# Down product of an expert layer: the 64-row half in three products of 128 rows, two of them stacked

## The reference

```python
gu = jnp.einsum('ech,eoh->eco', xb, gate_up_proj)     # 48 experts, 192 slots of 512
g, u = jnp.split(gu, 2, axis=-1)                      # 192 and 192
h = jax.nn.silu(g) * u
out = jnp.einsum('eci,ehi->ech', h, down_proj)        # 192 slots x 512
...
final = jnp.zeros_like(x).at[tok].add(y * w[:, None])
```

## Time and profile before

| what | value |
|---|---|
| runs | 1069.98, 1064.69, 1068.07 us; median 1068.07 |
| the profiled execution | 1064.81 us, of which the span from first to last instruction is 1063.1 |
| busy over the span | PE 96%, DVE 79%, ACT 59%, POOL 53% |
| mean granted TensorE clock | 0.986 of full speed |
| down products L1426, high x low, 128-row left side | 391 ns each |

### The profile page before, as it was taken

How to read it: one execution, slowest core, us unless ns; L and a number is a source line. 1 busy time by engine, 2 the same in 40 slices (tenths; PEclk the granted TensorE clock), 3 DMA queues, 4 the chain that set the end, 5 groups by cost and what they waited for, 6 DMA issues and landing times.

```text
span 1063.1 us, 24370 instructions
## 1 busy us (share of the span) xinstructions
PE 1016.1 (96%) x6564; PEld 835.6 (79%) x6564; DVE 835.3 (79%) x2255; ACT 624.7 (59%) x1751; POOL 560.9 (53%) x565
## 2 busy tenths in 40 slices
PE   5999799999999999999999997899999999999994
PEld 4787687887887887887877875688888888888883
DVE  5777587887887887888888876378888888888883
ACT  4555455555545545545555553177777777777772
POOL 3225466566567666666666666623443434434334
PEclk9999899999999999999999999799999999999998
DMA  7999584453331221211311514168999999999995
GB/s 274 376 306 254 209 292 183 145 213 138 101 116 50 77 72 50 87 61 50 98 50 50 210 40 159 41 207 236 255 261 248 263 251 256 262 241 263 252 224 69
DMA packets 90644, 185.75 MB, mean 175 GB/s; under 512 B 23943, under 2 KB 24071, under 8 KB 89712
## 3 DMA queue, kind: packets, MB, share of 16 engines
q1 hardware_dynamic: 59232, 145.13, 42.6%
q0 software_dynamic: 31376, 40.20, 16.8%
HBM read 116.04 MB, written 122.00 MB: 224 GB/s over the span
## 4 chain that ended last, share of the span: by engine, by line
PE 54%; issue 13%; POOL 13%; DMA 9%; DVE 8%; ACT 1%; SPq 1%; DVEq 1%; POOLq 0%; ACTq 0%
PE ps L1236 15%; PE ps L1392 14%; PE ps L1426 9%; POOL slot_records L594 7%; PE ps L1221 5%; DMA arena<-in_x 4%; PE ps L1408 3%; PE ps L1226 3%; POOL rstd L605 2%; DVE qk_both L1058 2%; DMA arena<-slot_records 2%; DMA layer_out<-qk_both,slot_table 2%; POOL arena L650 1%; PE ps L1334 1%; PE ps L1263 1%
## 5 line engine op out<-in xcount | busy, mean ns | idle before, releaser
L594 POOL DMA_INDIRECT slot_records<-row,slot_idx x240 | 243.3, 1014 | 80.2 <-issue 50.8
L679 POOL DMA_INDIRECT layer_out<-qk_both,slot_table x96 | 145.1, 1511 | 218.2 <-DMA layer_out<-qk_both,slot_table 190.7
L605 POOL TENSOR_TENSOR rstd<-mv,neg_half 128x1 f32<-128x1 f32 x96 | 67.8, 706 | 125.5 <-DVE mv L976 78.6
L1236 PE MATMUL ps<-w_high,xn_high 128*128 128x512 f32 x384 | 114.1, 419 | 0.7 <-ACT xn_high L700 0.7
L735 ACT ACTIVATE arena<-ps,neg_max 128x128 f32<-128x128 f32 x256 | 89.9, 377 | 31.9 <-DVE neg_max L968 31.9
L1236 PE MATMUL ps<-w_high,xn_low 128*128 128x512 f32 x384 | 107.3, 401 | 0.0
L1236 PE MATMUL ps<-w_low,xn_high 128*128 128x512 f32 x384 | 107.2, 401 | 0.0
L700 ACT ACTIVATE xn_t<-ps 128x512 f32<-128x512 f32 x64 | 38.3, 599 | 100.8 <-PE ps L1221 100.7
L1392 PE MATMUL ps<-w_high,w_low 128*128 128x192 f32 x576 | 87.8, 274 | 0.0
L1392 PE MATMUL ps<-w_low,w_high 128*128 128x192 f32 x576 | 87.7, 274 | 0.0
L1392 PE MATMUL ps<-w_high 128*128 128x192 f32 x576 | 86.8, 272 | 0.4 <-DVE w_low L1143 0.4
(11 more groups left out here) (164 smaller groups left out, 2468.5 us busy)
## 6 DMA issues: line engine op xcount, KB each, us to landing
gu_sb<-in_gate_up SPq DMA_DIRECT2D x48, 768.0 KB, 5.4
slot_records<-arena SPq DMA_DIRECT2D x6, 3366.0 KB, 25.1
arena<-slot_records SPq DMA_DIRECT2D x48, 280.5 KB, 4.8
dn_sb<-in_down_proj SPq DMA_DIRECT2D x48, 256.0 KB, 5.4
arena<-in_x SPq DMA_DIRECT2D x32, 256.0 KB, 2.7
x_res<-in_x SPq DMA_DIRECT2D x32, 256.0 KB, 3.0
ctx_t_sb<-in_ctx_t SPq DMA_DIRECT2D x32, 256.0 KB, 3.5
ctx_sb<-in_ctx_rows SPq DMA_DIRECT2D x32, 256.0 KB, 4.0
```

The lines of the kernel that those rows point to most:

```text
L594: pool.indirect_dma_start(out=records, out_offset=bass.IndirectOffsetOnAxis(ap=slot_idx_of(s)[:, k:k + 1], axis=0), in_=row_of(s), in_offs ...
L605: pool.tensor_tensor(rstd[:, :], mv[:, 1:2], neg_half[:, 0:1], ALU.pow).then_inc(steps.sem, 1)
L679: pool.indirect_dma_start(out=out, out_offset=bass.IndirectOffsetOnAxis(ap=slot_table[0:PART[h], 2 * d.index + h:2 * d.index + h + 1], axi ...
L1236: last = pe.matmul(dst, left[:, c, :], right[:, m, c, :], start=(n == 0 and c == 0), stop=(n == 2 and c == KC - 1))
```

## The change

Three things change, all in the expert stage.

- **Products.** The second half of the down product takes three products instead of five. `h1_low` and a second copy of the last 64 columns of `h1_high` lie side by side, as do the high and low parts of `h2`, and 128 columns that reach across the seam (`MIXED`) are the left side. So the product with `dn_high` gives low x high in the rows 0 to 63 of bank 5 and high x high in the rows 64 to 127. The two halves of that bank must be added. ScalarE scales the rows 64 to 127 into a spare part of `y` (`y1_rest`), and VectorE scales the rows 0 to 63 and adds them (`scalar_tensor_tensor`).
- **Copies.** ScalarE writes the 64 columns of `h1_high` a second time (`high1_again`), VectorE subtracts the low part of `h2` in two pieces, and copies the 64 slot weights to the rows 64 to 127.
- **Order.** The split of the 64-row down weights (ScalarE's `dn2_high`, VectorE's `dn2_low`) moves from the end of the turn in which the expert is `u` to the turn in which it is `d`, between the first and the second silu.

```diff
@@ -243,16 +243,20 @@
+                                  (P, 2, 1, 2 * CAP + P)):
+        gu_high, rows_high, dn_high, dn2_both, h1_parts = split_buffers(w_high)
+        gu_low, rows_low, dn_low, _, h2_parts = split_buffers(w_low)
+        LEFT = (slice(2 * CAP - P, 2 * CAP), slice(CAP, 2 * CAP - P))
+        MIXED = slice(P, 2 * CAP - P)
         HALVES = (slice(0, INTER - P), slice(INTER - P, P))
+        h1_low, h1_high_again = h1_parts[:, :, :, 0:CAP], h1_parts[:, :, :, CAP:2 * P]
+        h1_high = h1_parts[:, :, :, 2 * P:2 * P + CAP]
+        h2_high, h2_again = h2_parts[HALVES[0], :, :, 0:CAP], h2_parts[HALVES[1], :, :, 0:CAP]
@@ -809,6 +813,13 @@
                     if u.back(1).exists():
                         act.wait_ge(gup_v.sem, gup_v.after(u.back(1), "h2"))
                     act.activation(silu1[:, :], ps[:, 2, 0:CAP], ACT.Silu).then_inc(gup_a.sem, 1)
+                if d.exists():
+                    if d.first():
+                        act.wait_ge(d_dn2, 16 * 3)
+                    if d.back(2).exists():
+                        act.wait_ge(dwn_t.sem, dwn_t.after(d.back(2), "y1"))
+                    copy(dn2_high(d), dn2_raw(d), wdn_a)
+                if u.exists():
                     act.wait_ge(gup_t.sem, gup_t.after(u, "second"))
                     act.activation(silu2[:, :], ps[0:INTER - P, 3, 0:CAP], ACT.Silu).then_inc(gup_a.sem, 1)
                 if t.exists():
@@ -824,6 +835,8 @@
                     for h, dst, name in ((h1, h1_high, "h1"), (h2, h2_high, "h2")):
                         act.wait_ge(gup_v.sem, gup_v.after(u, name))
                         copy(dst[:, u.parity, 0, :], h[:, :], gup_a)
+                        if name == "h1":
+                            copy(h1_high_again[:, u.parity, 0, :], h1[:, P:CAP], gup_a)
                     copy(h2_again[:, u.parity, 0, :], h2[:, :], gup_a)
                 if d.exists():
                     act.wait_ge(dwn_t.sem, dwn_t.after(d, "y0"))
@@ -831,16 +844,16 @@
                     if d.back(2).exists():
                         act.wait_ge(d_add[d.back(2).parity], moved(d.back(2), 2))
                     copy(y[:, d.parity, 0, :], ps[:, 4, :], dwn_a, scale=weight_of[d.parity][:, 0:1])
+                    act.wait_ge(dwn_t.sem, dwn_t.after(d, "y1"))
+                    copy(y[PART[1]:P, d.parity, 1, :], ps[PART[1]:P, 5, :], dwn_a,
+                         scale=weight_of[d.parity][PART[1]:P, 1:2])
                 if n.exists():
                     split_gate_up(n)
                 if u.exists():
                     act.wait_ge(d_dn[u.parity], moved(u, 1))
-                    if u.first():
-                        act.wait_ge(d_dn2, 16 * 3)
                     if u.back(2).exists():
                         act.wait_ge(dwn_t.sem, dwn_t.after(u.back(2), "y1"))
                     copy(dn_high[:, u.parity, 0, :], dn_sb[:, u.parity, :], wdn_a)
-                    copy(dn2_high(u), dn2_raw(u), wdn_a)
             expert_turns(act, expert_turn)
 
         @block.vector
@@ -1151,6 +1164,10 @@
                         dve.wait_ge(gup_v.sem, gup_v.after(u.back(1), "low2"))
                         dve.wait_ge(gup_a.sem, gup_a.after(u.back(1), "again"))
                     dve.tensor_tensor(h1[:, :], silu1[:, :], ps[:, 2, CAP:2 * CAP], ALU.mult).then_inc(gup_v.sem, 1)
+                if d.exists():
+                    dve.wait_ge(wdn_a.sem, wdn_a.after(d, "high2"))
+                    left_by(dn2_low(d), dn2_raw(d), dn2_high(d)).then_inc(wdn_v.sem, 1)
+                if u.exists():
                     dve.wait_ge(gup_a.sem, gup_a.after(u, "silu2"))
                     dve.tensor_tensor(h2[:, :], silu2[:, :], ps[INTER - P:P, 3, 0:CAP], ALU.mult)\
                         .then_inc(gup_v.sem, 1)
@@ -1170,20 +1187,24 @@
                     dve.wait_ge(gup_a.sem, gup_a.after(u, "high2"))
                     if u.first():
                         for parity in range(2):
-                            dve.memset(h2_rest[HALVES[1 - parity], parity, 0, :].bitcast(FP32), 0.0)
-                    left_by(h2_low(u), h2[:, :], h2_high[:, u.parity, 0, :]).then_inc(gup_v.sem, 1)
-                if d.exists():
-                    dve.wait_ge(dwn_t.sem, dwn_t.after(d, "y1"))
-                    dve.wait_ge(ffn_w.sem, ffn_w.after(d, "weight"))
-                    if d.back(2).exists():
-                        dve.wait_ge(d_add[d.back(2).parity], moved(d.back(2), 2))
-                    dve.tensor_scalar(y[0:PART[1], d.parity, 1, :], ps[0:PART[1], 5, :],
-                                      weight_of[d.parity][0:PART[1], 1:2], None, ALU.mult).then_inc(dwn_v.sem, 1)
+                            dve.memset(h2_parts[HALVES[1 - parity], parity, 0, CAP:2 * CAP].bitcast(FP32), 0.0)
+                    for h in range(2):
+                        left_by(h2_low(u, h), h2[:, part(h)], h2_high[:, u.parity, 0, part(h)]).then_inc(gup_v.sem, 1)
                 if t.exists():
                     dve.wait_ge(d_rows[t.parity], moved(t, 2))
                     dve.tensor_copy(slot_table[:, bass.ds(2 * t.index, 2)],
                                     rows[:, t.parity, :, TOKEN:ROW].bitcast(I32).rearrange("p h o -> p (h o)"))\
                         .then_inc(ffn_w.sem, 1)
+                if d.exists():
+                    dve.wait_ge(dwn_a.sem, dwn_a.after(d, "y1_rest"))
+                    dve.wait_ge(dwn_t.sem, dwn_t.after(d, "y1"))
+                    dve.wait_ge(ffn_w.sem, ffn_w.after(d, "weight"))
+                    if d.back(2).exists():
+                        dve.wait_ge(d_add[d.back(2).parity], moved(d.back(2), 2))
+                    dve.scalar_tensor_tensor(y[0:PART[1], d.parity, 1, :], ps[0:PART[1], 5, :],
+                                             weight_of[d.parity][0:PART[1], 1:2], y[PART[1]:P, d.parity, 1, :],
+                                             ALU.mult, ALU.add).then_inc(dwn_v.sem, 1)
+                if t.exists():
                     if t.back(2).exists():
                         dve.wait_ge(dwn_a.sem, dwn_a.after(t.back(2), "y0"))
                         dve.wait_ge(dwn_v.sem, dwn_v.after(t.back(2), "y1"))
@@ -1191,6 +1212,9 @@
                     dve.tensor_copy(weight_of[t.parity][:, :],
                                     rows[:, t.parity, :, bass.ds(t.index + DM, 1)]
                                     .rearrange("p h o -> p (h o)")).then_inc(ffn_w.sem, 1)
+                    dve.wait_ge(ffn_w.sem, ffn_w.after(t, "weight0"))
+                    dve.tensor_copy(weight_of[t.parity][PART[1]:P, 1:2],
+                                    weight_of[t.parity][0:PART[1], 1:2]).then_inc(ffn_w.sem, 1)
                 if n.exists():
                     dve.wait_ge(wgu_a.sem, wgu_a.after(n, "high"))
                     if n.back(2).exists():
@@ -1201,8 +1225,6 @@
                     dve.wait_ge(wdn_a.sem, wdn_a.after(u, "high"))
                     left_by(dn_low[:, u.parity, 0, :], dn_sb[:, u.parity, :], dn_high[:, u.parity, 0, :])\
                         .then_inc(wdn_v.sem, 1)
-                    dve.wait_ge(wdn_a.sem, wdn_a.after(u, "high2"))
-                    left_by(dn2_low(u), dn2_raw(u), dn2_high(u)).then_inc(wdn_v.sem, 1)
             expert_turns(dve, expert_turn)
 
         @block.tensor
@@ -1419,12 +1441,18 @@
                         else:
                             if d.back(1).exists():
                                 pe.wait_ge(dwn_v.sem, dwn_v.after(d.back(1), "y1"))
-                        dst = ps[0:PART[h], 4 + h, :]
-                        pairs = [(h1_high, dn_high, P), (h1_high, dn_low, P), (h1_low, dn_high, P),
-                                 (h2_twice, dn2_both, P), (h2_rest, dn2_both, P)]
-                        for i, (left, right, n) in enumerate(pairs):
-                            last = pe.matmul(dst, left[0:n, d.parity, 0, part(h)], right[0:n, d.parity, 0, :],
-                                             start=(i == 0), stop=(i == len(pairs) - 1))
+                        e = d.parity
+                        if h == 0:
+                            steps = [(P, h1_high[:, e, 0, 0:P], dn_high), (P, h1_high[:, e, 0, 0:P], dn_low),
+                                     (P, h1_low[:, e, 0, 0:P], dn_high), (P, h2_parts[:, e, 0, 0:P], dn2_both),
+                                     (P, h2_parts[:, e, 0, LEFT[0]], dn2_both)]
+                        else:
+                            steps = [(P, h1_parts[:, e, 0, MIXED], dn_high),
+                                     (PART[1], h1_high[:, e, 0, P:CAP], dn_low),
+                                     (P, h2_parts[:, e, 0, MIXED], dn2_both)]
+                        for i, (n, left, right) in enumerate(steps):
+                            last = pe.matmul(ps[0:n, 4 + h, :], left, right[:, e, 0, :],
+                                             start=(i == 0), stop=(i == len(steps) - 1))
                         last.then_inc(dwn_t.sem, 1)
             expert_turns(pe, expert_turn)
 
```

16 lines of the change are left out of this document (6 added, 10 removed).

## The result

The changed kernel takes 1115.74 us (median of six runs, 1111.82 to 1117.23); the kernel before takes 1067.12 beside it (six runs, 1063.59 to 1069.98). The ratio is 1.045, with a 95% interval from 1.042 to 1.048: slower, as forecast, but by 48.6 us and not by 11. The time lies outside the predicted range.

The account below looks back on a forecast made before the run. A loop through D, down products, y1_rest and VectorE's subtractions, at 7.67 us, overtakes TensorE's pace: 45 x (7.67 - 7.353) = +14.3, + 0.4 - 3.5 = +11.2 us, giving 1079 us, 1.0% slower; range 1071 to 1097.

Parts of the forecast that it names:

- D: The moment VectorE ends the low part of the 64-row down weights; the prediction counts a turn's times from it.
- The first rival: Expert stage: TensorE's pace holds, the turn falls to 6.87 us and the time to 1046 us, faster; chance 8%.
- Two products fewer: TensorE's down products: two fewer at 0.23 us each save 0.46 us a turn; wider products cost nothing more.
- The release times: Waits between engines: the first down product starts 0.05 us after D, VectorE's gate-up subtraction 0.03 after ScalarE's split.
- the choice of the route: Ahead of VectorE's gate-up subtraction: ScalarE's split allows its start at 4.30 us, VectorE's own way at 4.22; ScalarE's taken.
- The spare of 0.31: Kernel before: the loop through D needs about 7.0 us against TensorE's 7.33, leaving about 0.31 us spare a turn.
- `y1_rest` from 2.20 to 2.89: ScalarE's added scaling takes 0.69 us, the next instruction starting after 0.59, so the gate-up split starts at 2.79.
- the predicted 7.67: Expert stage: the length in us of one turn of the loop after the change, against 7.353 before.
- The moved split: VectorE's turn end: gate-up subtraction 1.68 us, down subtraction 0.61, silu product 0.39 now in the loop, D's instruction 0.69.
- The end: Last additions into the output: POOL works off its lag in slower turns, 20.4 us instead of 24.0, a gain of 3.5.
- the loop is longer: Third rival, expert stage: short waiting VectorE instructions or TensorE's clock at 1.2 GHz make turns 8.2 us, 1103 us; chance 6%.

Follow-up runs that it names:

- e3: The changed kernel without ScalarE's y1_rest and the wait for it, rows 64 to 127 of bank 5 left out of the result: 1068.01 us, ratio 1.003.
- e10: The changed kernel with turns 24 to 47 of the expert stage written out with constants, turns 6 to 23 left in the hardware loop: 1097.97 us, ratio 1.028.
- e4: The changed kernel with only the order of waits changed ahead of the down products, y0 and y1, the last-released wait checked last: 1090.08 us, ratio 1.023.
- e2: The kernel before, its products kept, with only the split of the 64-row down weights moved between the silus: 1072.48 us, ratio 1.007.
- the last kernel: The changed kernel with down-weight split at turn's end, gate-up work ahead of y1, late waits last, all but two turns written out: 1077.18 us, ratio 1.009.

## Why the prediction was wrong in its size

*The bound and the direction: right.* TensorE's two products fewer gave nothing, and the loop through D, `y1_rest` and VectorE's subtractions became the bound. The first rival (1046) did not come. The rule that stood beside it, in the Trainium skill's "Perfetto Trace Analysis", section "Identifying the Most-Contended Engine", would have had the relief of the busiest engine pay; it did not pay here: the engine at 99.79% was relieved by 0.46 us a turn and the turn grew by 1.1. That is no test of the rule, since no run relieves TensorE without lengthening the loop; even without `y1_rest` (`e3`) the moved split and the copies are left, and the turn is 7.47.

*Two products fewer: right.* Behind the first step they stand 0.23 apart, 1.72 us from the first to the eighth (802.72, 804.44), and the wider ones are no slower.

*The release times: the step that failed.* "On release it starts 0.05 after D" was taken from the earlier trace rows, and the 0.03 between ScalarE's split and VectorE's subtraction from the earlier trace rows. Both are rows of written-out turns. In the hardware loop the same releases take 0.34 (TensorE) and 0.22 (VectorE's `y1`). `e10` shows both values in one trace, `e4` that the order of the waits alone changes them. What follows is that the gate-up subtraction starts at D + 4.94 and not at D + 4.30. With it the choice of the route failed: "ScalarE's is later and I take it" holds in the written-out turn, but in the loop each wait on VectorE adds to VectorE's own way (0.22 ahead of `y1`, 0.24 ahead of the weight copies), and that way, put at 4.22, ends at D + 4.91 while the split ends at D + 4.87. ScalarE adds its part, too: `y0` starts 1.62 behind the first product in the loop and 1.46 in the written-out turn. The spare of 0.31 was a misreading of the same kind: the product at 1036.79 in the earlier trace rows, of expert 45, is the first one behind the loop, where the release is short and the 0.36 is mostly spare. In the turns of the loop the step has nearly the same length (801.75 - 801.40 = 0.35), but there the release takes 0.34 of it. `e2` puts the true spare at 0.06.

*`y1_rest` from 2.20 to 2.89, with the next start after 0.59: too short.* It takes 0.69 as estimated, and in the written-out turn it ends at 948.95, D + 2.91. But the split starts 0.02 behind that end, at D + 2.93, and not 0.10 ahead of it at 2.79: the 0.59 of the earlier trace rows was taken from two instructions that both start in row 0, while `y1_rest` works on the rows 64 to 127 between two that start in row 0. The kernel before already shows the difference, in two of its turns (L700 on `arena` works on the rows 0 to 63 for an even expert and on the rows 64 to 127 for an odd one):

```profile
805.44 0.62 ACT L700 ACTIVATE w_high<-dn_sb 128x512 fp32r<-128x512 f32 x1
805.96 0.62 ACT L700 ACTIVATE w_high<-arena 64x512 fp32r x1
...
1032.97 0.62 ACT L700 ACTIVATE w_high<-dn_sb 128x512 fp32r<-128x512 f32 x1
1033.62 0.63 ACT L700 ACTIVATE w_high<-arena 64x512 fp32r x1
```

With the same start row the second starts 0.10 before the end of the first (805.96 against 806.06), with another start row 0.03 behind it (1033.62 against 1033.59). This is most of the 7.80 of `e10` beside the predicted 7.67. The prediction weighed the change of start rows for VectorE and not for ScalarE.

*The moved split: right.* From the gate-up subtraction on, 1.68, 0.60, 0.38 and 0.69 were measured for 1.68, 0.61, 0.39 and 0.69. The rule of the Trainium skill's "VectorE: DVE Perf Modes", section "Two Vector instructions with no wait between them", by which an instruction that starts in another group of 32 rows is held until those before it have finished, agrees: with the same start rows the silu product starts 809.60 - 809.00 = 0.60 after a subtraction of 0.69, with other ones D's subtraction starts 0.38 after a silu product of 0.34.

*The end: wrong.* The gain of 3.5 us did not come. POOL still waits for its own additions (206.7 us in 40 waits), the additions behind expert 45 are issued 1089.60 - 1085.84 = 3.76 after the end of `y0`, and from there to the end it is 1110.0 - 1085.84 = 24.16 us against 24.0 before. In the kernel before expert 45's were issued 1042.83 - 1039.12 = 3.71 after its `y0`, so the slower turns let POOL work nothing off: its additions became slower with the turn. Why was not tried.

*The rivals.* The third one, "the loop is longer", is the nearest to what came, but only in part by its mechanisms. The falls of the clock it names gave 5 us. Of the short VectorE instructions that wait for the one before, the wait of 0.24 ahead of the weight copies is in the loop, 0.11 more than in the written-out turn. The slow releases on TensorE, ScalarE and VectorE, the largest part, it does not name. It had 6% and 8.2 us a turn; the loop alone takes 8.36.

The sum, against the profiled execution (1111.82 against the predicted 1076.0, 35.8 more): the loop's releases 45 x (8.36 - 7.80) = 25.2, the overlap on ScalarE that isn't there, 45 x (7.80 - 7.67) = 5.9 (what the written-out turn already has), the falls 5.0, the end 3.7, less 3.1 for a first `y0` that ends at 704.87 + 0.69 = 705.56, that much earlier than forecast: 36.7. The 0.9 too much fits the first and last turns, which are written out and mostly shorter than 8.36. The 3.1 says nothing of the change: in the traces here the first down product starts anywhere between 702.8 and 708.3.

What stays open: which part of the release is the checking of the waits and which is work on registers, since `e4` changed the order and `e10` both the waits' form and the registers; why the clock fell in these four turns and not in others with the same waits; and what binds the last kernel.

## What to carry to other kernels

Take the time from a release to the start of an instruction from the turns that repeat, never from the written-out ones at the ends: 0.05 there was 0.34 in the loop, and a loop through three engines pays such a time at each crossing. Take the step from one instruction to the next from a pair with the same start rows: 0.59 became 0.71 where they change. Before a step is put between two engines, count what is queued behind it: `y1_rest` takes 0.69 us and cost 0.9 a turn, of which moving the queue out of its way gave back 0.6 without any change to the work. And where several semaphores stand ahead of one instruction, check the one that comes last at the end; that alone was worth 26 us here. Where an engine's own work is the bound it should give nothing, as writing the turns out gave nothing to the kernel before; the order of the waits was not tried there.

## What the runs showed of the hardware

- Inside the hardware loop TensorE starts 0.34 us after the last of four waits is released when that wait is checked first, 0.05 and 0.15 in alternate turns when it is checked last, and 0.05 in written-out code.
- ScalarE starts an instruction 0.10 us before the end of the one ahead when both start in the same row (805.96 against 805.44 + 0.62), and 0.02 to 0.03 behind that end when the start row changes (1033.62 against 1032.97 + 0.62; 805.76 against 804.34 + 1.40).
- VectorE starts an instruction that waits for its own one before it through a semaphore 0.24 us after that one's end in the loop (806.94 behind 805.96 + 0.74) and 0.13 in written-out code (949.85 behind 948.98 + 0.74).
- TensorE's granted clock fell to 0.50 in 4 of some 45 turns that all had waits of 1.3 to 1.5 us ahead of the down products, for 3.4 us each.
